# Two constant rows side by side in the array: the wave stages' bias product on 64 of TensorE's rows

## The reference, cut to what matters

```python
h = (cos(ph) + sin(ph)) * amp                    # 4 x 512 x 256
for l in range(2):
    ent = (h @ ent_w[l] + ent_b[l]) @ ent_pw[l] + ent_pb[l]
    h = layer_norm(h + ent, ln3_g[l], ln3_b[l])
    t = einsum('bsd,pdf->pbsf', h, path_w[l]) + path_b[l]
    interf = sum over p of t * (cos(phase[l]) + sin(phase[l]))
    h = layer_norm(h + interf, ln4_g[l], ln4_b[l])
```

## Time and profile before

| what | value |
|---|---|
| median of 3 runs | 1035.62 us (1034.5 to 1036.26) |
| span of the profiled execution | 1033.4 us |
| PE busy | 991.0 us, 96% of the span |
| DVE, ACT, POOL busy | 735.9, 606.6, 371.4 us |
| wave stages' linears, first and last start | 327.5 and 400.4 us |
| constants' products (line 1790) | 64, 278 ns each in the records |

### The profile page before, as it was taken

The page is one execution under the profiler, slowest core; times in us unless marked ns, Lnnn a source line. Parts: engine busy times, 40 slices in busy tenths (PEclk is TensorE's granted clock), DMA queues, the critical chain, the costliest instruction groups (busy, mean ns, idle before and its releaser), DMA issues.

```text
span 1033.4 us, 18254 instructions
## 1 busy us (share of the span) xinstructions
PE 991.0 (96%) x6658; PEld 826.1 (80%) x6658; DVE 735.9 (71%) x2003; ACT 606.6 (59%) x1177; POOL 371.4 (36%) x646
## 2 busy tenths in 40 slices
PE   8999999989999898889999999999999999999997
PEld 6555655556658897778989999999999999999997
DVE  6676787767638779866557777766776876677764
ACT  5576657664359774455556666455666655466660
POOL 4455474562131574353722223322222232222600
PEclk9899999998999999999999999999999999999999
DMA  7100010012110001022201010010101011010101
GB/s 249 28 2 22 4 35 8 23 60 85 45 65 4 1 8 36 28 76 62 82 1 42 1 41 4 39 42 1 42 1 42 1 42 42 1 42 1 42 24 59
DMA packets 29234, 36.91 MB, mean 36 GB/s; under 512 B 1780, under 2 KB 26584, under 8 KB 29144
## 3 DMA queue, kind: packets, MB, share of 16 engines
q1 hardware_dynamic: 24728, 31.15, 9.5%
q10 hardware_dynamic: 4416, 4.59, 1.4%
HBM read 31.40 MB, written 4.20 MB: 34 GB/s over the span
## 4 chain that ended last, share of the span: by engine, by line
PE 56%; DVE 4%; POOL 2%; issue 1%; ACT 1%; DVEq 0%; POOLq 0%; ACTq 0%
PE ps L1947 25%; PE ps L1964 24%; PE ps L1837 2%; PE ps L1919 2%; DVE ln_stats L2366 1%; PE ps L1977 1%; PE ps L1888 1%; POOL hs L1734 1%; POOL x_b L1734 0%; PE ps L1851 0%; DVE amp L2402 0%; PE ps L1866 0%; PE ps L1879 0%; PE ps L1788 0%; DVE att L2458 0%
## 5 line engine op out<-in xcount | busy, mean ns | idle before, releaser
L2202 ACT ACTIVATE G<-ps,bias_col 128x512 f32<-128x512 f32 x192 | 135.9, 708 | 176.6 <-PE ps L1947 167.9
L1964 PE MATMUL ps<-w_h,G_h 128*128 128x256 f32 x736 | 204.3, 278 | 0.0
L1964 PE MATMUL ps<-w_l,G_h 128*128 128x256 f32 x736 | 204.0, 277 | 0.0
L1964 PE MATMUL ps<-w_h,G_l 128*128 128x256 f32 x736 | 204.0, 277 | 0.0
L2506 DVE TENSOR_TENSOR G_l<-G,G_h 128x512 fp32r<-128x512 f32 x192 | 155.8, 820 | 59.6 <-ACT G_h L2203 59.6
L1764 POOL TENSOR_TENSOR x_a<-xn,mlp_g 128x1024 f32<-128x1024 f32 x20 | 68.0, 3399 | 333.8 <-DVE xn L2534 333.8
L708 ACT ACTIVATE probs<-ps 128x512 f32<-128x512 f32 (+3 forms) x256 | 98.3, 441 | 96.5 <-PE ps L847 95.7
L1947 PE MATMUL ps<-xT_h,w_h 128*128 128x512 f32 x384 | 151.7, 395 | 0.2 <-issue 0.2
L1947 PE MATMUL ps<-xT_h,w_l 128*128 128x512 f32 x384 | 149.9, 390 | 0.0
L1947 PE MATMUL ps<-xT_l,w_h 128*128 128x512 f32 x384 | 149.5, 389 | 0.0
L1124 DVE CUSTOM_DVE_ANT_0 ps<-ps,q_mask 128x128 f32<-128x128 f32 (+3 forms) x256 | 120.8, 512 | 29.5 <-PE ps L836 29.0
(11 more groups left out here) (330 smaller groups left out, 2099.8 us busy)
## 6 DMA issues: line engine op xcount, KB each, us to landing
w_raw<-L_ffn_W_T SPq DMA_DIRECT2D x12, 1024.0 KB, 5.1
hs<-L_attn_hidden_states SPq DMA_DIRECT2D x8, 512.0 KB, 3.9
x_kept<-hs SPq DMA_DIRECT2D x4, 512.0 KB, 4.1
w_raw<-x_kept SPq DMA_DIRECT2D x2, 1024.0 KB, 5.3
out<-xn SPq DMA_DIRECT2D x3, 512.0 KB, 2.8
w_raw<-L_ffn_ent_w_T SPq DMA_DIRECT2D x1, 1024.0 KB, 9.8
w_raw<-L_ffn_ent_pw SPq DMA_DIRECT2D x1, 1024.0 KB, 12.0
heads_T<-neg_rows SPq DMA_DIRECT2D x64, 2.0 KB
```

Of the source, the lines that this page charges most:

```text
L1964: mm = pe.matmul(ps[:, 4 + t // 2, (t % 2) * D:(t % 2 + 1) * D], x[b % 2][f][:, t * P:(t + 1) * P], w2_chunk(w, f), start=(k == 0), stop=( ...
L2202: act.activation(G32[n % 4], bank, ACT.Gelu, bias=bias)
```

## The change

Three edits. The product of the constant row contracts over 64 rows in place of 128: for two of the four tiles over rows 0 to 63 of `sel` and `stage_c_hl`, for the other two over rows 64 to 127. The tiles go in the order 0, 2, 1, 3; after the twelve products of a pair of tiles, (0, 2) or (1, 3), their two constants' products stand one after the other. The tiles of a pair lie in different banks. For that, `sel` gets ones in rows 64 and 96 as well (GpSimd: two more memsets, and a wait after each), and rows 96 to 127 of `stage_c_hl` get the low parts (VectorE: two more subtractions). TensorE's wait for g_zero asks for 5.

```diff
-        for n in range(2):
-            rows = g.stage_c_hl[32:64, n:STAGES:2, :]
-            ins = v.tensor_tensor(rows, g.stage_c[32:64, 1 - n:STAGES:2, :], rows.bitcast(F32), ALU.subtract)
+        for at in (32, 96):
+            for n in range(2):
+                rows = g.stage_c_hl[at:at + 32, n:STAGES:2, :]
+                ins = v.tensor_tensor(rows, g.stage_c[at:at + 32, 1 - n:STAGES:2, :], rows.bitcast(F32), ALU.subtract)
         ins.then_inc(g.wave["v_c"], 1)
...
-        for row in (0, 32):
+        for n, row in enumerate((0, 32, 64, 96)):
             pool.memset(sel[row:row + 1, :].bitcast(F32), 1.0).then_inc(wave["g_zero"], 1)
-
-        pool.wait_ge(wave["g_zero"], 3)
+            pool.wait_ge(wave["g_zero"], n + 2)
...
-            for t in range(RT):
-                n = 0
-                for c in range(KC):
-                    for x, w in ((g.xT_h, g.stage_w_h), (g.xT_h, g.stage_w_l), (g.xT_l, g.stage_w_h)):
-                        pe.matmul(banks(b)[t], x[:, b, c, t * P:(t + 1) * P], w[:, st, c, :], start=(n == 0), stop=False)
-                        n += 1
-                mm = pe.matmul(banks(b)[t], sel, g.stage_c_hl[:, st, :], start=False, stop=True)
+            for pair in ((0, 2), (1, 3)):
+                for t in pair:
+                    n = 0
+                    for c in range(KC):
+                        for x, w in ((g.xT_h, g.stage_w_h), (g.xT_h, g.stage_w_l), (g.xT_l, g.stage_w_h)):
+                            pe.matmul(banks(b)[t], x[:, b, c, t * P:(t + 1) * P], w[:, st, c, :], start=(n == 0), stop=False)
+                            n += 1
+                for t, rows in zip(pair, (slice(0, SLOT), slice(SLOT, P))):
+                    mm = pe.matmul(banks(b)[t], sel[rows, :], g.stage_c_hl[rows, st, :], start=False, stop=True)
             mm.then_inc(wave["p_lin"], 1)
...
-        pe.wait_ge(wave["g_zero"], 3)
+        pe.wait_ge(wave["g_zero"], 5)
```

## The result

The changed kernel takes 1039.21 us in the median of 5 runs (1038.58 to 1040.12), against 1035.62 us before (5 runs). The ratio is 1.0038, 95% interval 1.0026 to 1.0050: slower by 3.6 us, between 2.7 and 5.2.

The account below looks back on a forecast made before the run. TensorE was taken to bound stages 1 and 2: eight linears at +0.47 us less 0.77 of waits gave +2.99, with +0.33 at the last p_lin +3.3, taken as +3.4. Forecast 1039.0 us, range 1038.2 to 1040.2.

Parts of the forecast that it names:

- The bound: TensorE limits up to 378.34 us, then waits twice for ScalarE; its slack between 349.2 and 384 is 0.77 us.
- The price of a pair: In each linear: first pair +0.26 us, second +0.21, so TensorE needs 0.47 us more instead of 0.24 less.
- Entry: From the last full product to the 64-row pair: 0.20 us where 0.118 is usual.
- exit: From the 64-row pair to the next full product: 0.31 us.
- the load: First full product behind a pair carries its own weight load, so the next starts 0.22 us behind it.
- the turn's first load: Behind a linear's second pair, the break costs a turn's 8 transposes 0.05 us.
- The chain: Eight linears, less two waits: +2.99 us at the turn at 383.34; then +0.33 at stage 3 batch 0's p_lin.
- What was put at nothing: Stage 0, stage 3's batches 1 to 3, added subtractions and memsets, tile order: no delay; either stage at most 0.5 us.
- A: Rival, 6%: the pair overlaps and the array changes shape for nothing; each linear 0.236 us shorter, 1034.2 us.
- B: Rival, 12%: shape changes cost, but the pair's loads are drawn ahead; +0.11 us per pair, +1.2 in all, 1036.8 us.
- C: Rival, 7%: the relay from 384 to 490 us swallows the delay; 1035.6 to 1037 us.
- D: Rival, 5%: breaks thin out TensorE's work and its clock falls to 1.2 GHz in the wave stages; 1041.6 us.

Follow-up runs that it names:

- the kernel with four changes of shape: Against the kernel before: a single 64-row constants' product behind each tile's six, old tile order, no pairs, side work as in the change; 1051.57 us, ratio 1.0154.

## Why the prediction was right

*The bound.* Right: stages 1 and 2 run at TensorE's pace, stage 0 is covered by its wait, stage 3 counts once. The three kernels with pairs in some stages show it: 0.1, 3.2 and 0.4 us.

*The price of a pair.* Right in each term. Entry 0.20 against a measured 0.21, exit 0.31 against 0.31 or 0.32, the load 0.22 against 0.22 or 0.23, the turn's first load 0.05 against 1.09 - 1.04. Rounding took 0.01 off the entry, twice in a linear, and a few thousandths off each of the others: a linear with its turn costs 4.68 - 4.16 = 0.52 us more, not 0.47. That is why the sum of the rounded rows, +3.3, fell short of the trace's +3.61; the +3.4 taken was nearer. One slip worked the other way: the sum charges the 0.05 us to the turns behind all eight linears, but the last two, at 378.89 and 383.34, had waited and took 1.09 us already, which makes it 0.1 us too high. So +3.3 came as near as it did partly because these two errors offset each other.

*The chain.* Predicted +2.99 at the last turn of the eight linears; measured (388.00 - 350.56) - (383.34 - 349.15) = +3.25. Predicted +0.33 for p_lin behind it; measured (392.79 - 388.00) - (387.77 - 383.34) = +0.36. The waits of 0.55 and 0.22 us were eaten up, as taken.

*What was put at nothing.* Stage 0, the memsets, the order: nothing, each shown by a kernel. VectorE's two more subtractions: nothing, shown. Stage 3's other three linears: nothing here; the kernel with four changes of shape shows that this cover ends somewhere below 1.5 us a linear.

*The rivals.* A (the shape changes for nothing) falls by the rows at 354.71 to 355.24, and so does what the Trainium skill's page "TensorE: Matmul & The Clock Gate", Part 3, would give if it stood alone: its 4 ns between two row groups agree with the trace, where a pair lasts 0.38 us and a single one, at 369.77 in the kernel with four changes, lasts 0.38 us too, but the entry and exit outweigh what that saves. B (loads drawn ahead) falls by the load at 354.92, which waits for no semaphore and still starts with its matmul. C falls by the 92.26 us behind the relay. D did not come about in the wave stages: the stretch from 349.2 to 405 us ran at 1.00 throughout. Falls of the clock did come, at 295 and 461 us among others, at places that the prediction did not name; the first is no consequence of the change, and whether the second, which the changed kernel had in neither profile, hangs on a delay is open.

## What to carry to other kernels

A single pair of products on half of the array's rows, put between full ones, loses: here entry, exit and the load that is no longer drawn ahead take 0.74 us where three steps, 0.35 us, would do if the pair went by in the flow as one product. That is 0.39 us lost, and a pair of 256 columns saves 0.118. By these numbers, as an estimate that no run here tests, more than three such pairs would have to follow each other before the change of shape pays. Before a product is given another shape, look in the trace for the same kernel's places where the shape changes, and read the starts, not the lengths. Then ask of each stage whether its engine has a wait to lose: the same pairs cost 3.2 us in two stages and nothing in a third.

## What was not expected of the hardware

Full products of 256 columns ran at two paces: mostly 0.118 us from start to start, but 0.113 in some stretches. In the kernel with the constants first on 64 rows a linear's 24 products held one pace throughout, and many linears had the fast one (above, 367.93 to 368.04). Over 24 products that is 0.1 us, and it is why that kernel's period grew by 0.06 us in most linears: the linear behind the turn at 353.54 ran at 0.118, with a period of 4.34 us, the next one at 0.113, with 4.22. The kernel before has the fast pace too, and there it changed within the flow: six steps from 354.37 to 355.05 took 0.113 us each, and from the product behind the first constants' product on, with no break between, they took 0.118. What sets the pace no run here tells.
